# Scaling the skip rows at a batch's seventh quad, transfers of the last tiles in their own space with their sums on Pool, and one bank's sum ahead of a split

## The reference, cut to what matters

```
x  = layernorm(x)                       # 8 batches of 512 rows, 512 columns
s  = state-space branch(x)              # kept in s_scratch
h  = rmsnorm(x, ln2_w)
gate = silu(h @ W_in_base.T + mod * (h @ A) @ B)   # mod = 0.1 * tanh(attention(..) @ A)
up   = h @ W_up_base.T
ffn  = x + gate * up @ W_down.T
out  = x_in + s * silu(ffn)
```

## Time and profile before

| | |
|---|---|
| median of 3 runs | 2501.05 us (2500.99 to 3898.19) |
| profiled execution | 2505.93 us, its span 2503.4 us |
| PE busy | 2399.7 us, 96% |
| DVE, ACT, Pool busy | 1485.3, 1106.6, 699.7 us |
| mean granted clock of TensorE | 0.986 |

### The profile page before, as it was taken

How to read it: one execution, slowest core, us unless ns; L and a number is a source line. 1 busy time by engine, 2 the same in 40 slices (tenths; PEclk the granted TensorE clock), 3 DMA queues, 4 the chain that set the end, 5 groups by cost and what they waited for, 6 DMA issues and landing times.

```text
span 2503.4 us, 37640 instructions
## 1 busy us (share of the span) xinstructions
PE 2399.7 (96%) x13847; PEld 1943.7 (78%) x13847; DVE 1485.3 (59%) x3007; ACT 1106.6 (44%) x1895; POOL 699.7 (28%) x667
## 2 busy tenths in 40 slices
PE   7999999999999899999999897999999999999997
PEld 5888878878788677777777686788788888888785
DVE  7856657667656688888888742222222245454545
ACT  6444544544444477777777621111111233333332
POOL 4000000000001255444444507464647102021210
PEclk9999999999999999999999998999999999999998
DMA  4000100000003677676667134655555946555551
GB/s 145 18 34 1 34 19 16 35 17 18 17 18 107 203 213 209 194 205 191 188 191 206 56 138 162 201 189 192 185 189 170 354 178 210 193 202 202 193 210 67
DMA packets 190748, 348.66 MB, mean 139 GB/s; under 512 B 19008, under 2 KB 89664, under 8 KB 181840
## 3 DMA queue, kind: packets, MB, share of 16 engines
q1 hardware_dynamic: 188064, 345.91, 42.0%
q10 hardware_dynamic: 2496, 0.29, 0.1%
HBM read 234.70 MB, written 111.15 MB: 138 GB/s over the span
## 4 chain that ended last, share of the span: by engine, by line
PE 76%; DVE 7%; DMA 5%; issue 5%; ACT 2%; POOL 2%; SPq 2%; DVEq 0%; ACTq 0%; POOLq 0%
PE PS L72 12%; PE PS L74 11%; PE PS L73 11%; PE PS L1748 2%; PE PS L813 2%; PE PS L812 2%; PE PS L814 2%; PE PS L1706 2%; PE PS L2247 2%; PE PS L2248 2%; PE PS L2249 2%; PE PS L1725 2%; PE PS L1707 2%; PE PS L1708 2%; PE PS L2587 2%
## 5 line engine op out<-in xcount | busy, mean ns | idle before, releaser
L1912 DVE CUSTOM_DVE_ANT_0 PS<-PS,MK 128x512 f32<-128x512 f32 (+3 forms) x512 | 244.2, 503 | 70.9 <-PE PS L1725 69.5
L1848 ACT ACTIVATE PF<-PS 128x512 f32<-128x512 f32 (+1 forms) x384 | 200.6, 527 | 91.7 <-PE PS L1752 61.3
L72 PE MATMUL PS<-XH,WH 128*128 128x512 f32 x504 | 208.9, 415 | 0.0
L2296 DVE TENSOR_TENSOR SG<-SG,PS 128x512 f32<-128x512 f32 x60 | 41.1, 686 | 267.3 <-PE PS L74 266.1
L74 PE MATMUL PS<-XH,WL 128*128 128x512 f32 x504 | 197.8, 392 | 0.0
L73 PE MATMUL PS<-XL,WH 128*128 128x512 f32 x504 | 197.1, 391 | 0.0
L74 PE MATMUL PS<-FH,GU 128*128 128x512 f32 x480 | 188.1, 392 | 0.0
L73 PE MATMUL PS<-FL,GU 128*128 128x512 f32 x480 | 187.9, 392 | 0.0
L72 PE MATMUL PS<-FH,GU 128*128 128x512 f32 x480 | 187.9, 391 | 0.0
L1725 PE MATMUL PS<-KS,QS 96*128 96x512 f32 (+3 forms) x512 | 171.3, 349 | 16.6 <-DVE MX L1912 16.4
L72 PE MATMUL PS<-XB,SW 128*128 128x512 f32 x448 | 175.4, 392 | 3.7 <-ACT P L2644 3.7
(11 more groups left out here) (350 smaller groups left out, 6687.7 us busy)
## 6 DMA issues: line engine op xcount, KB each, us to landing
SW<-sw_scratch SPq DMA_DIRECT2D x10, 3584.0 KB, 12.2
qk_scratch<-QT SPq DMA_DIRECT2D x128, 256.0 KB, 4.6
QS<-qk_scratch SPq DMA_DIRECT2D x96, 256.0 KB, 4.0
KS<-qk_scratch SPq DMA_DIRECT2D x96, 256.0 KB, 4.0
xt_scratch<-JOB SPq DMA_DIRECT2D x32, 512.0 KB, 3.7
XB<-xt_scratch SPq DMA_DIRECT2D x16, 1024.0 KB, 6.7
sw_scratch<-JOB SPq DMA_DIRECT2D x32, 448.0 KB, 3.2
DW<-dw_scratch SPq DMA_DIRECT2D x10, 1024.0 KB, 4.9
```

What stands on the lines that cost most here:

```text
L72: pe.matmul(o, lh(k), xh(k), start=open_ and k == 0, stop=False, skip_group_check=True)
L1848: act.activation(PE_[u][:, o:o + at], PS[4 + a % 2][:, 0:at], ACT.Exp, scale=SC).then_inc(a_ex, 1)
L1912: dve.tensor_tensor_reduce(out=p, in0=p, in1=MK[:, 512 - n:512], scale=1.0, scalar=NEG, op0=ALU.add, op1=ALU.max, accum_out=MX[w % 2][:, j ...
```

## The change

Three places in `ffn_order` and the second half; what is computed is the same.

1. The step "skips" stays at f = 1 for SP; DVE's scaling is a step of its own, "skips_scaled", at f = 6, behind the product of that quad. For batch 0 it moves from ahead of the modulation to quad 6.
2. Tiles 4 to 7 of the last pair get buffers ENDS of their own, in the space of the blocks XB1 and XB2, which the last unit has read with its sixth product; SP loads them then, all eight transfers in a row. In the last unit DVE multiplies tile i - 2 behind eviction i; Pool adds tiles 0 to 6 and DVE tile 7. SP no longer issues loads between the last writes.
3. In every unit DVE adds bank ZG to P1 ahead of the split of G21 into HH, not behind it.

```diff
@@ ffn_order
                 if f == 1 and b:
                     yield "skips", b
+                if f == 6:
+                    yield "skips_scaled", b
@@ ffn_vector
-                elif kind == "skips":
+                elif kind == "skips_scaled":
@@ buffers and loads
+        es = ExitStack()
+        sb(es, "KEPT2", [128, 8584])
+        ENDS = sb(es, "ENDS", [128, 8, DM])
+        es.close()
+        def end_tiles(n):
+            if n < 8 * PAIRS - 4:
+                return STR[n % 4][:, :], XTR[n % 4][:, :]
+            return ENDS[:, n % 4, :], ENDS[:, 4 + n % 4, :]
+        def ends_landed(n):
+            if n < 8 * PAIRS - 4:
+                return n_xs[n % 4], n_xs0[n % 4] + 32 * (n // 4 + 1)
+            return n_xb[3 + n % 4], n_xb0[3 + n % 4] + block_landed(PAIRS - 1, 3 + n % 4) + 32
@@ written
-                sp.wait_ge(n_fa, n_fa0 + 8 * p + i + 1)
+                if 8 * p + i < 8 * PAIRS - 1:
+                    sp.wait_ge(n_fa, n_fa0 + 8 * p + i + 1)
+                else:
+                    sp.wait_ge(n_hl, 4 * V_ + 1)
                 sp.dma_start(on_[8 * p + i], MP[i][:, :]).then_inc(n_mt[i], 16)
-                if i < 4:
+                if i < 4 and p + 1 < PAIRS:
                     load_ends(sp, 8 * p + i + 4)
@@ second_sync, ahead of the last written()
+            sp.wait_ge(n_pr, 15 * V_ - 9)
+            for i in range(4, 8):
+                load_ends(sp, 8 * PAIRS - 8 + i)
@@ second_vector
                 finish(v, 6)
+                dve.wait_ge(n_pr, c + 9)
+                dve.tensor_tensor(P1[0][:, :], P1[0][:, :], ZG[:, :], ALU.add).then_inc(n_ad, 1)
                 dve.wait_ge(n_hh, 4 * v + 1)
                 dve.tensor_tensor(HH[:, 1, 0, 1, :], G21[:, :], f32(HH[:, 1, 0, 0, :]), ALU.subtract).then_inc(n_hl, 1)
-                dve.wait_ge(n_pr, c + 9)
-                dve.tensor_tensor(P1[0][:, :], P1[0][:, :], ZG[:, :], ALU.add).then_inc(n_ad, 1)
...
                 for i in range(1, 8):
                     evict(v, i)
-            for i in range(8):
+                    if v == V_ - 1 and i >= 2:
+                        finish(V_, i - 2)
+            for i in range(6, 8):
                 finish(V_, i)
-                dve.wait_ge(n_fm, n_fm0 + 8 * PAIRS - 8 + i + 1)
-                dve.tensor_tensor(MP[i][:, :], MP[i][:, :], XTR[i % 4][:, :], ALU.add).then_inc(n_fa, 1)
+            dve.wait_ge(n_fm, n_fm0 + 8 * PAIRS)
+            dve.tensor_tensor(MP[7][:, :], MP[7][:, :], end_tiles(8 * PAIRS - 1)[1], ALU.add).then_inc(n_hl, 1)
@@ second_pool
+            for n in range(8 * PAIRS - 8, 8 * PAIRS - 1):
+                skipped(n)
```

More of the change, by code:

```diff
@@ L2455, in load_partial @@
             sp.dma_start(MP[i][:, :], mn_[n]).then_inc(n_mt[i], 16)
+        def end_tiles(n):
[6 more added lines that the diff above has]
+            return n_xb[3 + n % 4], n_xb0[3 + n % 4] + block_landed(PAIRS - 1, 3 + n % 4) + 32
         def load_ends(sp, n):
-            sp.dma_start(STR[n % 4][:, :], sn_[n]).then_inc(n_xs[n % 4], 16)
-            sp.dma_start(XTR[n % 4][:, :], xn_[n]).then_inc(n_xs[n % 4], 16)
+            scale, skip = end_tiles(n)
+            sp.dma_start(scale, sn_[n]).then_inc(ends_landed(n)[0], 16)
+            sp.dma_start(skip, xn_[n]).then_inc(ends_landed(n)[0], 16)
         def second_ahead(sp):
@@ L2669, in finish @@
                     dve.wait_ge(n_fs, n_fs0 + n + 1)
-                    dve.wait_ge(n_xs[n % 4], n_xs0[n % 4] + 32 * (n // 4 + 1))
-                    dve.tensor_tensor(MP[i][:, :], MP[i][:, :], STR[i % 4][:, :], ALU.mult).then_inc(n_fm, 1)
+                    dve.wait_ge(*ends_landed(n))
+                    dve.tensor_tensor(MP[i][:, :], MP[i][:, :], end_tiles(n)[0], ALU.mult).then_inc(n_fm, 1)
             def evict(v, i):
@@ L2720, in second_vector, with skipped @@
                     evict(v, i)
-            for i in range(8):
+                    if v == V_ - 1 and i >= 2:
+                        finish(V_, i - 2)
+            for i in range(6, 8):
                 finish(V_, i)
-                dve.wait_ge(n_fm, n_fm0 + 8 * PAIRS - 8 + i + 1)
-                dve.tensor_tensor(MP[i][:, :], MP[i][:, :], XTR[i % 4][:, :], ALU.add).then_inc(n_fa, 1)
+            dve.wait_ge(n_fm, n_fm0 + 8 * PAIRS)
+            dve.tensor_tensor(MP[7][:, :], MP[7][:, :], end_tiles(8 * PAIRS - 1)[1], ALU.add).then_inc(n_hl, 1)
         def second_pool(pool):
+            def skipped(n):
+                pool.wait_ge(n_fm, n_fm0 + n + 1)
+                pool.wait_ge(*ends_landed(n))
+                pool.tensor_tensor(MP[n % 8][:, :], MP[n % 8][:, :], end_tiles(n)[1], ALU.add).then_inc(n_fa, 1)
             for v in range(V_):
                 if v and v % UNITS == 0:
[L2729 to L2733, removed]
+                    for n in range(2 * v - 8, 2 * v):
+                        skipped(n)
                 pool.wait_ge(n_cp, 8 * v + 7)
```

## The result

The changed kernel takes 2480.72 us in the median (2479.31 to 2481.08, 4 runs). The kernel before took 2500.99, 2501.05 and 2508.28 us beside it and, in one slow run that is left out here, 3898.19 us. By the medians of 2480.72 and 2501.05 the change saves 20.3 us, by the means (2480.46 and 2503.44) 23.0. The ratio is 0.9904, 95% interval [0.9884, 0.9924], which stands for 19 to 29 us, 24 in its middle; 30.7 were forecast. Later runs of the kernel before have medians of 2504.98 us (19 runs), 2504.77 (7) and 2502.13 (11), so 24 is nearer than 20.3. The time lies in the forecast's range of 2461 to 2483, near its upper end, 10.7 us above the 2470 named as likeliest and 0.7 above the 2464 to 2480 of its likeliest case.

The account below looks back on a forecast made before the run. TensorE, busy 2399.7 of 2503.4 us, was taken as the bound, so only its waits and the tail could be won. 24.3 + 0.6 + 0.1 + 5.7 = 30.7 us off the 2501.05 median gave 2470, range 2461 to 2483.

Parts of the forecast that it names:

- likeliest case: Whole kernel: the forecast's own case, 2464 to 2480 us, given a chance of 73%.
- Part 1: Scaling moved to the seventh quad: PE's three long quads return to 8.44 us, saving 24.3, plus 0.6 at L1953.
- the cover at the seventh quad: DVE's idle time and PE's later need of GL give some 10 us against some 5 us of scalings.
- SP's slack: End of batch 1: SP waited 24.2 us for DVE's M, of which 16.1 go.
- Part 2: Bank's sum ahead of the split: at pair borders the second wait takes back the first's gain; 0.1 us saved, bounds 0 and 1.8.
- ACT's earlier chain: At a border, silu of P1, silu of MP and copy P5 start 0.6 us earlier, cutting each 1.2 us wait by up to 0.6.
- Part 3: Tail behind PE's last matmul: earlier transfers and finishing, Pool's sums 1.92 us apart; 5.7 us saved, bounds 2.7 and 10.3.
- half-returned stall: First half: half of the scaling move's gain comes back as PE waits, giving 2482 us.
- The stall did not move to SP: Rival, 10%: SP behind Pool's jobs holds up row loads or writes of M, PE waits there; 2482 or 2494 us.
- Pool did not run freely in the tail: Rival, 12%: Pool runs freely in the tail, 4.6 us more saved, 2465.5 us.
- the scalings did not outgrow their cover: Rival, 2%: four scalings with the port taken by Pool outgrow 10 us of cover; time above 2501 us.
- hidden gain of 19 us: Rival, 3%: a gain over 2% needs 19 us no row shows, such as a shorter job chain on SP.

Follow-up runs that it names:

- e6: Kernel before, with SP issuing the XT loads a quad earlier, ahead of row loads and jobs, scaling left at the second quad: 2480.95 us, ratio 0.9907.
- e2: Kernel before with the third edit alone, bank ZG's sum ahead of the split of G21: 2506.74 us, ratio 1.0009.
- e4: Kernel before with the second edit alone, the last tiles' own buffers, finishing between evictions and Pool's sums: 2498.85 us, ratio 0.9972.
- e11: The changed kernel run once more as it is, on one chip: 2479.22 us, ratio 0.9901.
- e5: Changed kernel with the old order of split and sum, and all eight tail sums on DVE, none on Pool: 2474.53 us, ratio 0.9875.
- e3: Kernel before with the first edit alone, scaling at the seventh quad: 2481.3 us, ratio 0.9905.
- e8: Changed kernel with the old order of split and sum, tiles 6 and 7 of a pair finished behind the unit's last split: 2466.19 us, ratio 0.9844.
- e1: Changed kernel with its third edit undone, split of G21 again ahead of bank ZG's sum: 2476.84 us, ratio 0.9881.

## Why the prediction was right or wrong

**Part 1, 24.3 + 0.6 forecast: right in mechanism, and in size for the profile it was read from.** Between quad 4 and the first unit the profiles differ by 531.92 - 506.86 = 25.06 us: 24.27 from the three long quads, and 0.79 at L1953 (e6 shows the 0.79 by itself). The return of the clock was part of it: 18.7 us of waits gave 24.3. In e2 and e4 the two shorter waits left the clock at 1.00 and cost little more than their own length: waits of 1.40 and 2.41, 1.29 and 1.68 us made quads of 10.15 and 11.14, 10.03 and 10.42 us, each 0.3 us more than 8.44 and the wait. In the profile of before, with the clock at 0.50 behind them, it was 1.9 us more than 8.44 and the wait. Every condition that was named held: the cover at the seventh quad (4.73 us of scalings in the idle time), SP's slack (24.2 - 16.1 = 8.1 forecast, 7.3 measured), the landed loads. The size was that of one long stall, though: the executions that have the stall show 531.92, 529.65 and 527.08 (before, e2, e4), 22.7 us above 506.86 in the mean. The term was too large by 2.2 us of its 24.9, because the length of this stall was taken from one profile.

**Part 2, 0.1 us saved forecast: wrong in sign.** The measured cost is 2.1 us in the mean, 2.7 in the first profile. The step that failed is that the product of P1 "starts as soon as the other bank's sum is done, which does not move". It moved by up to 0.7 us, since the split now stood ahead of that sum with Pool's tile sum already under way. The lock was in the same prediction, two paragraphs further down and with the right number, but applied to the tail alone. The trace of before has the border's rows, DVE's multiply of tile 6 and split, then Pool's sum of tile 6:

```profile
2119.81 0.69 DVE L2671 TENSOR_TENSOR MP<-MP,STR 128x512 f32<-128x512 f32 x1 [1.70 <-DMA XTR<-in_x_dram]
2120.42 0.69 DVE L2690 TENSOR_TENSOR HH<-G,HH 128x512 fp32r<-128x512 f32 x1
...
2120.59 1.67 POOL L2733 TENSOR_TENSOR MP<-MP,XTR 128x512 f32<-128x512 f32 x1 [1.70 <-DVE MP L2671]
```

The split came 0.17 us ahead of Pool's sum and blocked it; an operation put between the two had to turn that round. The bounds, 0 and 1.8 saved, had no loss in them and no reason for leaving it out. Of the up to 1.8 us from ACT's earlier chain a part came: PE's first waits sum to 3.6 us after, 2.9 in e2 and 2.0 in e11, against 3.7 before. One gain was not in the sum at all: with the old order PE's modulation matmul of the border unit (L2516, the next one into bank ZG) waits for the moved sum itself in seven of the 18 border units, up to 1.02 us; with the new order in none of nine.

**Part 3, 5.7 us forecast, 6.7 measured.** Shifted by the 19.46 us by which the profile's evictions were earlier, the working put Pool's first sum at 2461.19 (measured 2461.20) and its fifth at 2468.8 (2468.87), period 1.92 (1.93). One step was off: I let Pool wait for both last multiplies. It got in between the second and the third of the last three multiplies, as the row of three multiplies in 3.65 us shows, and the third ended 0.55 us behind Pool's sum; so Pool's last two sums ended at 2474.1 instead of 2475.1. The rule of the Trainium skill (SBUF — State Buffer, "SBUF: two separate sides") that a DVE operation with two SBUF inputs and a GpSimd operation hold a shared pair of ports one at a time, for the whole instruction, is borne out by these rows. e5 shows what that makes of Pool's sums: without them the tail is 1.5 us shorter still.

**The base.** The sum was taken off 2501.05 us; more executions put the kernel before at 2502 to 2505, so 1 to 4 us of the 10.7 by which the time lies above 2470 are this. By the means of the stages the change is worth 22.7 - 2.1 + 6.6 = 27.2 us (tails: 17.8 before, 11.2 after), inside the interval of 19 to 29. The ratio's 24 is some 3 lower; that is less than the first column's spread, but where these 3 us are stays open.

**The signs.** PE's last matmul was to start 25 us earlier; it started 19.5 earlier (2466.10 against 2485.57), since the first column was 2.9 us longer and the units 2.7. The borders' waits were to be near 0.7 and 1.1 us; they were 1.2 and 1.5. The others held: 8.44 us throughout, no clock of 0.50, scalings without a wait, Pool's sums 1.9 us apart.

**The range.** The likeliest case, 2464 to 2480, was missed by 0.7 us. That the time lies in the range is owed to its upper end of 2483, which was set for a half-returned stall; no stall returned, so this part is luck.

**The rivals.** The stall did not move to SP, Pool did not run freely in the tail, the scalings did not outgrow their cover, and no hidden gain of 19 us came: the likeliest case held in its mechanisms, but for the border.

## What to carry to other kernels

A wait in an in-order engine costs what is queued behind it. Moving the waiting step to where its data have long been there (e3) or its load ahead in the queue (e6) gives the same, and the gain can exceed the wait, where the clock comes back too. Where two engines exclude each other, the order of two cheap operations decides who goes first: look at what the other engine starts in just that gap, also in edits that seem to be about something else. And finishing work that waits for transfers belongs behind the last thing that the busiest engine needs (e8), not among it; here that was worth 8.3 us of the units (504.5 to 496.2), more than the whole edit of the tail.

## What the runs showed of the hardware

- DVE and Pool operations on SBUF tiles exclude each other in each of the cases shown. A DVE operation with two SBUF tiles that takes 0.69 us alone ended 0.55 to 0.56 us after Pool's when it was blocked, whenever it was issued; a scaling (0.55 us alone) ended 0.28 us after. A DVE operation that reads a bank is neither blocked nor does it block (0.67 us beside Pool in the earlier trace rows; L2715 beside Pool's start at 2098.91).
- In a row of DVE operations at 0.60 us distance, a waiting Pool operation got its turn as soon as the running one ended, ahead of the next. Pool's last two sums took 3.31 us together, where one takes 1.29 alone.
- What a short wait costs PE depends on whether the granted clock falls behind it. Waits of 1.91 and 2.48 us with 0.50 behind them made quads 3.81 and 4.39 us longer than 8.44 (before); waits of 1.29, 1.40, 1.68 and 2.41 us that left it at 1.00 made them 1.59 to 2.70 us longer (e2, e4).
- The same short waits did not always have the same outcome. At the borders two waits close together, 0.69 and 1.24 us (e3), 0.30 and 1.24 (e4), 0.55 and 1.24 (e5), were followed by some 3.4 us at 0.50, while 1.02 and 1.24 (before), 0.67 and 1.24 (e1), 0.28 and 1.24 (e6) and all nine borders with the new order left the clock at 1.00.
